# Five edits to a transformer layer on eight cores: an engine swap for a PSUM copy, a third PSUM bank, a weight load in four pieces, and the last two layer norms' multiplies moved to GpSimd

## The reference, cut to what matters

```
h = layer_norm(x);  q, k, v = h@wq, h@wk, h@wv         # 4 heads of 256
q = softmax(q*s, over features);  k = softmax(k*s, over tokens)
attn = q @ (k^T v)                                     # linear attention
x1 = x + attn@wo + bo
x2 = x1 + gelu(layer_norm(x1)@w_ff1 + b_ff1)@w_ff2 + b_ff2
x3 = layernorm(x + x2@w_d + b_d)                       # outer norm, "L3"
f  = (silu(x3@wg.T) * (x3@wu.T)) @ wd.T                # int weights / 127
out = layernorm(x3 + f)                                # outer norm, "L4"
```

## Time and profile before

| | us |
|---|---|
| Median of 2 runs | 2078.87 (2077.93 to 2079.80) |
| The profiled execution's own time | 2077.03 |
| Its span on the slowest core (core 5) | 2075.2 |
| Spans of the 8 cores | 2061.7 to 2075.2 |
| TensorE matmul busy | 1648.1 (79%) |
| VectorE busy | 595.8 (29%) |
| ScalarE busy | 536.2 (26%) |
| GpSimd busy | 20.4 (1%) |

### The profile page before, as it was taken

The page is one execution under the profiler, slowest core; times in us unless marked ns, Lnnn a source line. Parts: engine busy times, 40 slices in busy tenths (PEclk is TensorE's granted clock), DMA queues, the critical chain, the costliest instruction groups (busy, mean ns, idle before and its releaser), DMA issues.

```text
span 2075.2 us, 20356 instructions; the slowest of 8 cores (2061.7 to 2075.2 us)
## 1 busy us (share of the span) xinstructions
PE 1648.1 (79%) x7096; PEld 680.4 (33%) x7096; DVE 595.8 (29%) x908; ACT 536.2 (26%) x834; POOL 20.4 (1%) x27
## 2 busy tenths in 40 slices
PE   1488888987558567999999956557999999998662
PEld 0133333442113112444444422112444444443220
DVE  1633333201214322403031223332323113212344
ACT  1233333222220555030302204444210110113222
POOL 0000000000000000000000000000000000000000
PEclk9998998998779667999999977667999999998675
DMA  9321110020082400222222051102006007000112
GB/s 188 82 59 41 41 41 1 1 41 0 0 192 66 66 0 0 41 41 41 41 41 41 1 122 41 41 0 41 0 15 108 1 1 122 1 1 1 41 41 81
DMA packets 45107, 89.57 MB, mean 43 GB/s; under 512 B 848, under 2 KB 3024, under 8 KB 45008
## 3 DMA queue, kind: packets, MB, share of 16 engines
q0 software_dynamic: 23920, 46.14, 13.9%
q1 hardware_dynamic: 21088, 42.13, 6.6%
HBM read 126.01 MB, written 8.39 MB: 65 GB/s over the span
## 4 chain that ended last, share of the span: by engine, by line
PE 52%; ACT 8%; DVE 8%; issue 2%; DMA 2%; DVEq 0%; ACTq 0%; POOLq 0%; SPq 0%
PE pb L793 11%; PE pb L819 11%; PE pb L1045 8%; PE pb L992 8%; PE pb L1002 8%; ACT sbb L623 3%; ACT sbb L625 3%; PE pb L703 3%; PE pb L913 3%; DMA slotD<-wdd 1%; DVE R L875 1%; DVE xq L960 1%; DVE R L879 1%; DVE R L956 1%; DMA estR<-xkv 1%
## 5 line engine op out<-in xcount | busy, mean ns | idle before, releaser
L1045 PE MATMUL pb<-Dr,wslotE 128*128 128x512 bf16 x768 | 184.9, 407 | 28.2 <-DVE R L1052 28.2
L992 PE MATMUL pb<-h2x,W 128*128 128x512 bf16 x768 | 185.8, 386 | 4.8 <-ACT slbt L1011 4.8
L1002 PE MATMUL pb<-h2x,W 128*128 128x512 bf16 x768 | 182.6, 381 | 0.0
L800 ACT ACTIVATE Gq<-pb,pv 128x512 bf16<-128x512 f32 x128 | 87.9, 687 | 301.7 <-PE pb L793 301.2
L1011 ACT ACTIVATE slbt<-pb 128x512 bf16<-128x512 f32 x96 | 57.3, 597 | 375.1 <-PE pb L992 371.7
L793 PE MATMUL pb<-h2x,W 128*128 128x512 bf16 x512 | 123.4, 405 | 38.7 <-ACT h2x L735 37.3
L1016 DVE SCALAR_TENSOR_TENSOR Dr<-slbt,pb 128x512 bf16<-128x512 bf16 x96 | 66.0, 687 | 281.2 <-PE pb L1002 260.1
L834 DVE TENSOR_TENSOR R<-R,pb 128x512 f32<-128x512 f32 x96 | 66.0, 687 | 265.5 <-PE pb L819 265.5
L415 PE MATMUL pb<-W,h 128*128 128x512 bf16 x512 | 128.7, 397 | 0.4 <-ACT ebf L423 0.4
L431 PE MATMUL pb<-slotD,h 128*128 128x512 bf16 x512 | 122.5, 382 | 0.0
L1045 PEld LDWEIGHTS pb<-Dr,wslotE 128*128 128x128 bf16 x768 | 78.6, 103 | 132.6 <-issue 64.0
(11 more groups left out here) (94 smaller groups left out, 1449.2 us busy)
## 6 DMA issues: line engine op xcount, KB each, us to landing
xq<-xkv SPq DMA_DIRECT2D x8, 2048.0 KB, 10.8
estR<-xkv SPq DMA_DIRECT2D x8, 2048.0 KB, 16.7
W<-wff POOLq DMA_DIRECT2D x4, 2048.0 KB, 22.9
slotD<-wff POOLq DMA_DIRECT2D x4, 2048.0 KB, 17.5
y<-xq SPq DMA_DIRECT2D x4, 2048.0 KB, 6.9
W<-wgT POOLq DMA_DIRECT2D x3, 2048.0 KB, 17.3
W<-wuT POOLq DMA_DIRECT2D x3, 2048.0 KB, 29.2
wslotE<-wdT POOLq DMA_DIRECT2D x3, 2048.0 KB, 22.2
```

Of the source, the lines that this page charges most:

```text
L800: se = b.op("scalar", lambda e, jj=jj, t=t, qq=qq, bk=bk: e.activation(Gq[:, jj * NOWN + t * NT: jj * NOWN + (t + 1) * NT], bk["ap"][:, :] ...
L992: b.op("tensor", lambda e, hc=hc, kc=kc, t=t, bA=bA: e.matmul(bA["ap"][:, :], W0[:, kc * 1024 + hc * 128: kc * 1024 + (hc + 1) * 128], h2x ...
L1002: b.op("tensor", lambda e, hc=hc, kc=kc, t=t, bB=bB: e.matmul(bB["ap"][:, :], W1[:, kc * 1024 + hc * 128: kc * 1024 + (hc + 1) * 128], h2x ...
L1045: b.op("tensor", lambda e, m=m, hc=hc, t=t, wds=wds, bk=bk: e.matmul(bk["ap"][:, :], wds[:, hc * 1024 + m * 128: hc * 1024 + (m + 1) * 128 ...
```

## The change

Five edits:
1. The four copies of the context into `Csb` go from VectorE to ScalarE.
2. `rot3`, the banks of the attention output stage, gets a third bank (bank 2).
3. The load of `w_d` is issued as four DMAs of 256 columns each in place of two of 512. Group m of the projection waits for piece m // 2.
4. In `l3_apply` the multiply by the reciprocal deviation goes to GpSimd. GpSimd reads no PSUM here: ScalarE first copies `lnS` into a new bf16 tile `rsgb` (in the space of `tmp1`). GpSimd's operations count on a new semaphore `gp2`. The ScalarE cast into `h2x` waits for GpSimd in place of VectorE, and bank 6 is free after the copy in place of after the last multiply.
5. The same in `l4_apply`, with the output slot as GpSimd's target; the store waits for GpSimd.

```diff
     for h in range(H):
-        ve = b.op("vector", lambda e, h=h: e.tensor_copy(
-            Csb[:, h * 512:(h + 1) * 512], pbs[h][:, :]),
-            waits=[("te", kv_te), ("te", p0_sbb_done)], inc="ve")
+        ve = b.op("scalar", lambda e, h=h: e.activation(
+            Csb[:, h * 512:(h + 1) * 512], pbs[h][:, :], AF.Identity),
+            waits=[("te", kv_te), ("te", p0_sbb_done)], inc="se")
...
-    rot3 = mkpool([0, 1])
+    rot3 = mkpool([0, 1, 2])
...
-    gd1 = gpQ.dma(lambda e: e.dma_start(
-        ap3(slotD1, 0, [[8192, 128], [1024, CH], [1, 512]]),
-        ap3(wdd_d, 0, [[D, 128], [128 * D, CH], [1, 512]])),
-        waits=[("te", q3b_done[0])])
-    gd2 = gpQ.dma(lambda e: e.dma_start(
-        ap3(slotD1, 512, [[8192, 128], [1024, CH], [1, 512]]),
-        ap3(wdd_d, 512, [[D, 128], [128 * D, CH], [1, 512]])),
-        waits=[("te", q3b_done[0])])
+    gds = [gpQ.dma(lambda e, q=q: e.dma_start(
+        ap3(slotD1, q * 256, [[8192, 128], [1024, CH], [1, 256]]),
+        ap3(wdd_d, q * 256, [[D, 128], [128 * D, CH], [1, 256]])),
+        waits=[("te", q3b_done[0])]) for q in range(4)]
...
     def l3_apply(t):
         ch = L3[t]
+        sc = b.op("scalar", lambda e: e.activation(
+            rsgb[:, :], lnS["ap"][:, :], AF.Identity),
+            waits=[("te", ch["bc_done"]), ("gp2", ln_state.get("rsgb_free", 0))],
+            inc="se")
...
-            b.op("vector", lambda e, c=c, t=t: e.tensor_mul(
+            gp = b.op("gpsimd", lambda e, c=c, t=t: e.tensor_mul(
                 R1[:, c * NOWN + t * NT: c * NOWN + (t + 1) * NT],
                 R1[:, c * NOWN + t * NT: c * NOWN + (t + 1) * NT],
-                lnS["ap"][:, :]), inc="ve")
+                rsgb[:, :]), waits=[("se", sc), ("ve", ve)], inc="gp2")
...
-                waits=[("te", q3a_done[0]), ("ve", b.cnt["ve"])], inc="se")
+                waits=[("te", q3a_done[0]), ("gp2", gp)], inc="se")
+        ln_state["rsgb_free"] = b.cnt["gp2"]
         Pool.rel(lnB_, "ve", b.cnt["ve"])
-        Pool.rel(lnS, "ve", b.cnt["ve"])
+        Pool.rel(lnS, "se", sc)
...
-            gd = gd1 if m < 4 else gd2
+            gd = gds[m // 2]
```

More of the change, by code:

```diff
@@ L38, in __init__ @@
         self.cnt = {}
-        for s in ("te", "ve", "se", "syA", "syB", "gpA", "gpB"):
+        for s in ("te", "ve", "se", "gp2", "syA", "syB", "gpA", "gpB"):
             self.sem[s] = self.es.enter_context(self.nc.semaphore(s))
@@ L181, in build_nc @@
     tmp1 = sbt("tmp1", [128, NT], F32)
+    rsgb = alias("rsgb", [128, NT], BF16, tmp1)
     rowb = sbt("rowb", [1, 2048], BF16)
@@ L575, in build_nc @@
                 for ec in range(2):
-                    w = (Pool.w(bk) + [("ve", cev[H - 1]), go]) if ec == 0 else []
+                    w = (Pool.w(bk) + [("se", cev[H - 1]), go]) if ec == 0 else []
                     b.op("tensor", lambda e, h=h, dc=dc, jh=jh, ec=ec, bk=bk: e.matmul(
@@ L873, in l3_apply @@
         ch = L3[t]
+        sc = b.op("scalar", lambda e: e.activation(
+            rsgb[:, :], lnS["ap"][:, :], AF.Identity),
+            waits=[("te", ch["bc_done"]), ("gp2", ln_state.get("rsgb_free", 0))],
+            inc="se")
         for c in range(CH):
-            b.op("vector", lambda e, c=c, t=t: e.tensor_sub(
+            ve = b.op("vector", lambda e, c=c, t=t: e.tensor_sub(
                 R1[:, c * NOWN + t * NT: c * NOWN + (t + 1) * NT],
@@ L878, in l3_apply @@
                 lnB_["ap"][:, :]), waits=[("te", ch["bc_done"])], inc="ve")
-            b.op("vector", lambda e, c=c, t=t: e.tensor_mul(
+            gp = b.op("gpsimd", lambda e, c=c, t=t: e.tensor_mul(
                 R1[:, c * NOWN + t * NT: c * NOWN + (t + 1) * NT],
                 R1[:, c * NOWN + t * NT: c * NOWN + (t + 1) * NT],
-                lnS["ap"][:, :]), inc="ve")
-            b.op("scalar", lambda e, c=c, t=t: e.activation(
+                rsgb[:, :]), waits=[("se", sc), ("ve", ve)], inc="gp2")
+            b.op("scalar", lambda e, c=c, t=t, gp=gp: e.activation(
                 h2x[:, c * NOWN + t * NT: c * NOWN + (t + 1) * NT],
@@ L954, in l4_apply @@
         xs = xsl[t % 2]
+        sc = b.op("scalar", lambda e: e.activation(
+            rsgb[:, :], lnS["ap"][:, :], AF.Identity),
+            waits=[("te", ch["bc_done"]), ("gp2", ln_state.get("rsgb_free", 0))],
+            inc="se")
+        gp = 0
         for c in range(CH):
-            b.op("vector", lambda e, c=c, t=t: e.tensor_sub(
+            ve = b.op("vector", lambda e, c=c, t=t: e.tensor_sub(
                 R1[:, c * NOWN + t * NT: c * NOWN + (t + 1) * NT],
@@ L959, in l4_apply @@
                 lnB_["ap"][:, :]), waits=[("te", ch["bc_done"])], inc="ve")
-            b.op("vector", lambda e, c=c, t=t, xs=xs: e.tensor_mul(
+            gp = b.op("gpsimd", lambda e, c=c, t=t, xs=xs: e.tensor_mul(
                 xs[:, c * NT:(c + 1) * NT],
                 R1[:, c * NOWN + t * NT: c * NOWN + (t + 1) * NT],
-                lnS["ap"][:, :]),
-                waits=[oslot_free[t % 2], ("te", r2a_done[0])], inc="ve")
+                rsgb[:, :]),
+                waits=[("se", sc), ("ve", ve), oslot_free[t % 2],
+                       ("te", r2a_done[0])], inc="gp2")
+        ln_state["rsgb_free"] = b.cnt["gp2"]
         Pool.rel(lnB_, "ve", b.cnt["ve"])
-        Pool.rel(lnS, "ve", b.cnt["ve"])
+        Pool.rel(lnS, "se", sc)
         ov = syQ.dma(lambda e, t=t, xs=xs: e.dma_start(
@@ L969, in l4_apply @@
             ap3(xs, 0, [[xs.shape[1], 128], [NT, CH], [1, NT]])),
-            waits=[("ve", b.cnt["ve"])])
+            waits=[("gp2", gp)])
         oslot_free[t % 2] = ov
```

## The result

The changed kernel takes 2016.55 us (median of 11 runs, 2012.79 at best) against 2077.52 us for the kernel before (10 runs). The ratio is 0.9718, with a 95% interval of 0.9684 to 0.9751: 59 us less. The forecast was 2032 in a range of 2013 to 2050, so 45 us of drop were named and 59 came.

What follows compares the result with a forecast made beforehand. The chain from VectorE's late evictions to ScalarE's statistics was taken to bound both norm stages, not TensorE. Terms -6.9-1.7+1-17.1-0.9-19.0-0.8 = -45.4 from 2077.0 gave 2032 us; its own range 2024 to 2046, the 8-in-10 range 2013 to 2050.

Steps and rivals of the forecast that it cites:

- The context copies: End of block PA: with the four copies on ScalarE, TensorE's 7.02 us stall before L577 goes; -6.9 us.
- The third bank: Attention output, block PB: one more matmul group runs at full clock under the wait for x; -1.7 us.
- The load of w_d in four: Projection by w_d: TensorE starts 2.8 us earlier, but late pieces lengthen the tile by 3.9; net +1 us.
- The fourth waits for the second: T+13.8 to T+19.3: Projection's w_d load: when the fourth piece lands, counted from T, TensorE's new start; T+16.5 taken, tile ending at T+20.
- The step of GpSimd: Both norm applies: time per GpSimd multiply, called p, bounded by 0.79 and 2.06 us, taken as 1.37.
- L3: Outer norm, tiles 0 to 2: each gains the smaller of 6.33 and 16.69-8p us, p being GpSimd's step; -17.1.
- Late next: Outer norm L3, tiles 0 to 2: after the change GpSimd is the late one, by half a microsecond.
- Norm L4: Norm L4, tiles 0 to 2: the full 6.33 us per tile come off whatever GpSimd's step p is; -19.0 us.
- Rival (a), the clock: L3 and L4: after shorter stalls each tile's last group runs at 2.4 GHz; total 2026, or 2019 with p=1.2; chance 0.20.
- (b): Norm applies: VectorE and GpSimd hinder each other, subtractions also take 1.37 us; total 2058; chance 0.11.
- (c): Projection: the fourth piece of w_d is late, by the high end of its range; total 2045; chance 0.08.
- (d): Norm applies: GpSimd becomes the bound through ScalarE's casts; slower beyond a step of 2.51 us, 2097 at 3.0; chance 0.06.

Runs made afterwards that it cites:

- experiment 1: The kernel before with only the four context copies moved from VectorE to ScalarE: 2064.92 us, ratio 0.9962 to the kernel before.
- experiment 2: The kernel before with only the third bank added in the attention output stage: 2071.79 us, ratio 0.9994 to the kernel before.
- experiment 6: The changed kernel with the load of x for tile 1 held until the fourth piece of w_d has landed: 2006.51 us, ratio 0.9679 to the kernel before.
- experiment 4: The changed kernel with each GpSimd multiply of the L3 apply done twice: ratio 0.9862 to the kernel before.
- experiment 5: The changed kernel with each GpSimd multiply of the L4 apply done twice: 2020.90 us, ratio 0.9749 to the kernel before.
- experiment 9: The changed kernel with each apply moved behind the next tile's last eviction and its multiplies on VectorE: 1988.06 us, ratio 0.9587 to the kernel before.

## Why the prediction was right, and where it was off

*What bounds it.* Right. The chain from VectorE's evictions to the statistics set the time of both norm stages, and the stages shrank by what was taken out of VectorE's list.

*The context copies.* Right: -7.0 against -6.9, and 7.5 us of the stage alone in experiment 1.

*The third bank.* The mechanism held in the tile it was worked out for: one more group under the wait, and tile 0 shorter by 1.8 us where 1.7 was taken. That the mean of the stage also moved by 1.7 is in part luck: single cores move by 3.4 us or not at all, and over all profiles the mean moves by 1.5 (experiment 2). On the slowest core's total it is not told from nothing.

*The load of w_d in four.* The first half held: a piece has 1024 packets whatever its width, the first matmul came 2.7 us earlier for 2.8 worked out, and experiment 6 confirmed the turns of the two queues with its 3.8 to 4.7 for 4.5. The failed step is "The fourth waits for the second: T+13.8 to T+19.3", with the middle taken. On core 5 the second, third and fourth piece landed at T+5.1, T+7.7 and T+11.6, the fourth at 11.6 to 12.9 on the eight cores. It was issued 5.6 us after the first matmul and landed 6.0 later, 3.6 of it its packets by the prediction's 56 ns, so 2.4 of latency where the high end had 9.1. The DMA view of the changed kernel for 1229 to 1240 us has that issue:

```profile
slotD<-wdd POOLq DMA_DIRECT2D x1, 512.0 KB, 6.0
```

Groups 7 and 8 are due at about T+12.1, so the piece is in time on core 5, where the 64 matmuls took 16.56 us in place of 16.09 all the same. Only on core 0 does TensorE wait for it, 0.8 us; cores 0 and 4 wait 0.3 and 0.9 us for the second piece. The tile is 0.4 us longer in the mean, where 3.9 was forecast. Of the 9.1 us read off the first piece of the kernel before, some 6 had passed when its first packets moved: between 1218 and 1222 us the DMA view has 21 of them, and the issue was at 1214.99. The fourth piece had nothing of x beside it. Whether that is why its latency is shorter is not shown. Net -2.3 for +1, an error of 3.3 us with the wrong sign.

*The step of GpSimd.* The term that was mis-sized: 1.37 was taken, 1.12 measured (8.96 over eight). With 1.12 in the formulas that stand there, L3 is -19.0 (the eviction path decides, since 1.12 is under 1.3), tile 3 is -2.9 and the last apply -2.8. That is 5.9 us of the 14.4 missing. The measured last apply is -2.7. The estimate of 1.12 us from the Trainium skill's GPSIMD Engine Reference (section 3.1) was the measured number. (With it the prediction's own formulas give a sum 5.9 us lower, not the "about 4" that stands beside it.) That page has VectorE faster by 1.96 for its longer operation; in this trace it is faster too, by less: 0.79 against 1.12 us a step is 1.4, and 0.687 against 1.15 of busy time 1.68.

*Late next.* "What is late next is GpSimd, by half a microsecond" did not hold at a step of 1.12: VectorE's eviction is last by 1.15 us. Experiment 4 shows that the formula behind it is right, with 23.4 us for 22.7.

*Norm L4.* "Whatever p is" held, at twice the step as well (experiment 5).

*Rival (a), the clock.* It came true in part, and with the step and the fourth piece it closes the sum: the L3 and L4 stages gained 2.2 us each and the rounds 0.8 beyond their terms, 5.2 of 14.4. The groups behind the stalls account for most of it. In the changed kernel's profile the 24 of L3 take 2.98 us in the mean and the 24 of L4 2.93, in place of 3.57 each; over three tiles that is 1.8 and 1.9 us a core. The last groups of the three tiles of L4 on core 5, and round 0's group behind the stall:

```profile
1898.22 3.49 PE L1054 MATMUL pb<-Dr,wslotE 128*128 128x512 bf16 x8 [2.35 <-DVE R L1061]
...
1937.62 1.89 PE L1054 MATMUL pb<-Dr,wslotE 128*128 128x512 bf16 x8 [2.30 <-DVE R L1061]
...
1975.46 2.50 PE L1054 MATMUL pb<-Dr,wslotE 128*128 128x512 bf16 x8 [2.42 <-DVE R L1061]
```

```profile
1437.32 1.89 PE L1001 MATMUL pb<-h2x,W 128*128 128x512 bf16 x8 [2.02 <-ACT slbt L1020]
```

After 9.6 and 4.8 us of stall these groups took 3.57 us each. After 2.0 to 2.4 us they took 1.89 to 3.49 here, and over all cores, after 1.5 to 3.4 us, 1.89 to 3.56: fast, slow or in between. I had treated the clock as one or the other.

*Rivals (b), (c), (d).* (b): the subtraction took 686 to 690 ns beside GpSimd, the same as alone. (c): the last groups were 0.4 us late in the mean, where the high end had the tile 13 us above the forecast. (d) needs a step over 2.5 and was produced only by doubling.

## What to carry to other kernels

When a matmul stalls for a free bank, read what stands in front of the eviction in the evicting engine's list. Moving that work to an idle engine pays what it takes out of the list; moving it behind the last eviction, under work that waits for nothing of it, pays more and needs no second engine, if the engine's idle time there is long enough (here 12.6 us under 13.1, experiment 9). A transfer that is needed much later should not be issued beside one that is waited for, since the queues share the DMA engines packet by packet (294 against 293 packets in 4 us); and cutting a load along its rows shortens the packets but not their number (1024 in a piece of either width here), so the first piece came only 2.7 us earlier.

## What the runs showed of the hardware that was not expected

- The feed-forward stage of 637 us takes one of two lengths, 3.4 us apart, on each core of each run, and a bank more shifts the odds, not the lengths. With three banks the length follows from whether tile 0's last eviction starts before 30.5 or after 32.0 us.
- A TensorE stall of 1.5 to 3.4 us leaves the following eight matmuls at 1.89 to 3.56 us (55 stalls on the eight cores of the changed kernel). In the kernel before, each of the 56 stalls of 4.8 to 9.6 us in the same places was followed by 3.57.
- GpSimd's multiply of 128x512 float32 by bf16 took 1141 to 1179 ns over all cores and kernels, also with bf16 output (experiment 4) and with VectorE at work on the same tile. Back to back its step was 1.12 us, shorter than the profile's own duration of one.
